# Rounding the next tile's rows earlier in the expert loop of a conv-attention-MoE kernel, and keeping its results later

## What is computed

```
router_logits = jnp.einsum('bsd,de->bse', x, Wg)
top_logits, top_idx = jax.lax.top_k(router_logits, TOP_K)      # TOP_K = 2
...
for e in range(E):                                             # E = 8
    h = jax.nn.silu(xt @ W1[e]) @ W2[e]                        # W1[e]: 128x512, W2[e]: 512x128
    out = out + cw[:, e:e + 1] * h
```

## Time and profile before

| | |
|---|---|
| median of three runs | 745.14 us (742.14 to 745.18) |
| profiled execution, its own time | 746.05 us |
| its span, first to last instruction | 744.2 us |
| TensorE matmul busy | 610.9 us (82%) |
| VectorE, ScalarE, GpSimd busy | 473.7, 306.3, 266.3 us |
| first matmul of the experts | 551.64 us |
| last scatter issued | 722.34 us |

### The profile page before, as it was taken

The page is one execution under the profiler, slowest core; times in us unless marked ns, Lnnn a source line. Parts: engine busy times, 40 slices in busy tenths (PEclk is TensorE's granted clock), DMA queues, the critical chain, the costliest instruction groups (busy, mean ns, idle before and its releaser), DMA issues. The chain is left out here.

```text
span 744.2 us, 11191 instructions
## 1 busy us (share of the span) xinstructions
PE 610.9 (82%) x3561; PEld 517.6 (70%) x3561; DVE 473.7 (64%) x1216; ACT 306.3 (41%) x615; POOL 266.3 (36%) x292
## 2 busy tenths in 40 slices
PE   5699999748699999989897997986229999999930
PEld 4588888535498898978796887875127777777720
DVE  5576795756558687857577686674305666666625
ACT  3221211242345363525344343432017777777810
POOL 3041553476000101321314141224632666666660
PEclk9899999859789999999899997887559999999985
DMA  8999434520441312130503122000177676777109
GB/s 263 386 362 334 170 133 165 177 92 1 141 142 54 89 60 83 57 115 5 167 1 126 46 85 87 19 12 25 37 236 244 215 234 210 228 224 235 62 5 337
DMA packets 56375, 105.47 MB, mean 142 GB/s; under 512 B 8872, under 2 KB 21817, under 8 KB 56192
## 3 DMA queue, kind: packets, MB, share of 16 engines
q1 hardware_dynamic: 51328, 96.24, 39.6%
q0 software_dynamic: 4992, 8.54, 3.3%
HBM read 58.15 MB, written 48.42 MB: 143 GB/s over the span
## 5 line engine op out<-in xcount | busy, mean ns | idle before, releaser
L1481 PE MATMUL bank<-rvx,s_expd 128*128 128x96 f32 x1024 | 139.5, 284 | 11.4 <-ACT s_expd L995 9.4
L1481 PEld LDWEIGHTS bank<-rvx,s_expd 128*128 128x128 f32 x1024 | 132.7, 202 | 14.5 <-ACT s_expd L995 11.3
L1744 POOL DMA_INDIRECT y_slots<-virt,pad_l x92 | 101.3, 1101 | 75.3 <-DVE virt L1795 47.5
L995 ACT ACTIVATE s_expd<-bank 128x512 f32<-128x512 f32 x128 | 75.7, 598 | 124.6 <-PE bank L1465 109.2
L1157 DVE TENSOR_REDUCE s_max<-bank 128x2 f32<-128x512 f32 x128 | 87.1, 689 | 57.3 <-PE bank L1444 44.7
L914 POOL DMA_INDIRECT x_slots<-rows,slot_of x64 | 62.7, 980 | 72.1 <-DVE rows L1284 48.2
L883 POOL TENSOR_TENSOR ln_rstd<-ln_var,power 128x4 f32<-128x4 f32 x16 | 16.4, 1022 | 199.0 <-DVE ln_var L1133 199.0
L1783 DVE TENSOR_TENSOR k_stack<-virt,k_stack 128x512 fp32r<-128x512 f32 x92 | 62.7, 688 | 18.1 <-ACT k_stack L1763 9.2
L53 PE MATMUL bank<-pad_h,u_h 128*128 128x512 f32 x144 | 60.9, 423 | 14.7 <-DVE pad_l L395 8.3
L1465 PE MATMUL bank<-q_stack,k_stack 100*128 100x256 f32 x256 | 62.4, 328 | 5.2 <-DVE q_stack L1175 5.2
L1763 ACT ACTIVATE k_stack<-virt 128x512 fp32r<-128x512 f32 x92 | 58.1, 632 | 2.9
(11 more groups left out here) (251 smaller groups left out, 1241.0 us busy)
## 6 DMA issues: line engine op xcount, KB each, us to landing
x_slots<-blank SPq DMA_DIRECT2D x8, 2112.0 KB, 20.4
pad_h<-w_split SPq DMA_DIRECT2D x23, 512.0 KB
q_stack<-w_split SPq DMA_DIRECT2D x23, 512.0 KB
qk_rows<-qk SPq DMA_DIRECT2D x16, 512.0 KB
k_stack<-qk_rows SPq DMA_DIRECT2D x96, 64.0 KB, 2.2
q_stack<-qk_rows SPq DMA_DIRECT2D x48, 128.0 KB, 2.4
pad_l<-x_slots SPq DMA_DIRECT2D x23, 264.0 KB
e_raw<-in_w SPq DMA_DIRECT2D x16, 256.0 KB, 3.0
```

The costliest lines, as they stand in the source:

```text
L995: nc.scalar.activation(expd[:, s % 2].rearrange("p a i -> p (a i)"), ps_st[s % 2][:, :], ACT.Exp).then_inc(exp_done, 1)
L1481: last = pe.matmul(ps_pv[s // 4][:, at:at + RVW], expd[:, s % 2, a, i * P:(i + 1) * P], rvx[:, ring, 2 * b + a, :], start=(a == 0), stop=( ...
L1744: pool.indirect_dma_start(out=y_slots[:, :], out_offset=bass.IndirectOffsetOnAxis(ap=ids, axis=0), in_=y_rows[:, t % 2, j, :], in_offset=N ...
```

## The change

Two orders are rewritten; TensorE's, GpSimd's and SyncE's stay as they are, and no operation is added or taken away. ScalarE rounds the rows of tile t+1 between silu(t, 1) and high(t, 1), where before it rounded those of tile t+2 after high(t, 1). VectorE's subtraction follows it. `keep_y(t - 1)` moves from behind low(t, 0) to ahead of low(t, 3). What stood behind low(t, 2) as `weigh(t - 1)` now stands one turn of the loop later, as `weigh(t - 2)` behind low(t, 1).

```diff
@@ ScalarE @@
         for t in range(NB):
             for f in range(FB):
                 silu(t, f)
+                if f == 1 and 1 <= t < NB - 1:
+                    z_split(t + 1)
                 high(t, f)
-                if f == 1 and t + 2 < NB:
-                    z_split(t + 2)
@@ VectorE @@
         for t in range(NB):
             for f in range(FB):
+                if f == 1 and 1 <= t < NB - 1:
+                    z_rest(t + 1)
+                if f == 3 and t:
+                    keep_y(t - 1)
                 low(t, f)
-                if f == 0 and t:
-                    keep_y(t - 1)
-                if f == 1 and t + 2 < NB:
-                    z_rest(t + 2)
-                if f == 2 and t:
-                    weigh(t - 1)
+                if f == 1 and t >= 2:
+                    weigh(t - 2)
+        weigh(NB - 2)
         keep_y(NB - 1)
         weigh(NB - 1)
```

## The result

The change takes 737.01 us in the median of four runs (735.71 to 738.04), the kernel before 745.16 in four (742.14 to 748.87). The ratio is 0.988, with a 95% interval of 0.985 to 0.991: 8.15 us faster, where 8.5 had been forecast. The profiled execution took 735.71 us, its span is 733.8.

What follows compares the result with a forecast made beforehand. TensorE was taken as the bound, with small holes where ScalarE waited for same-round transposes. Gains of 8.7 and 0.7 less 0.86 made 8.5 us, so 736.6 us, range 734.0 to 741.0 without the rivals.

Steps and rivals of the forecast that it cites:

- The chain: In expert rounds, ScalarE's wait for a same-round transpose delays silu, high and low, leaving TensorE holes of 0.33 and 0.30 us.
- The rounds: Rounds 1 to 20 of the experts: 6.40 us each without holes, 128.0 instead of 136.70, gaining 8.7 us.
- The start: Round 0 falls from 6.73 to about 5.9 to 6.0 us, gaining 0.7.
- I count nothing for that, at worst 0.5: Round 1's start may wait for the first moved rounding and its subtraction: counted as nothing, at worst 0.5 us.
- The tail: After the last rounds, weigh(20) comes later behind low(21, 1), delaying the twelve scatters and everything behind: 0.86 us lost.
- The sum: Whole kernel: 8.7 + 0.7 - 0.86 = 8.5 us gained, giving a median of 736.6 us.
- GpSimd as the bound: Experts' scatters all lengthened by colliding lows, 6.84 us a tile, making the kernel slower at 751.0 us; chance 0.04.
- Low(t, 3) behind the copy: VectorE's low(t, 3) stays late behind keep_y, a 0.30 us hole every round, only 2.5 gained, 742.6 us; chance 0.07.
- third rival: ScalarE stays in its old phase, subtraction ends late, each round's first product waits: slower, 760 us; chance 0.03.
- ScalarE's rest: ScalarE's line takes 5.48 us of a 6.40 us round, leaving 0.9 us of rest to catch up with.

Runs made afterwards that it cites:

- the other pattern of before: Unchanged kernel before, profiled again on another chip: every round 6.71 us, nineteen in 127.47 against 129.99 in the first profile; that execution took 723.7 us.
- the rounding alone: Kernel before with only ScalarE's rounding and VectorE's subtraction moved as in the change, keep_y and weigh left in place: 770.33 us, ratio to before 1.033.
- the results alone: Kernel before with only keep_y and weigh moved as in the change, rounding and subtraction left at tile t+2: 780.29 us, ratio to before 1.044.
- five more copies: The change plus five extra ScalarE copies into an unused buffer ahead of each rounding from tile 2 on: 737.81 us, ratio to before 1.024.

## Why the prediction was right

**The chain.** Shown. The step "ScalarE was made to wait for a transpose of the same round" is confirmed from both sides: the waits went from 23 to 2, and moving the same wait elsewhere, with the tile unchanged, brought rounds of 6.4 too, though not all. "That the rounding is one tile less ahead" was never the cause.

**The rounds.** 6.40 us were forecast, 6.41 came. The timeline of the change has the starts of rounds 0, 1 and 21, which answer to the earlier trace rows:

```profile
556.89 0.39 PE L53 MATMUL bank<-k_stack,pad_h 128*128 128x512 f32 x1
...
563.03 0.50 PE L53 MATMUL bank<-k_stack,pad_h 128*128 128x512 f32 x1
...
691.22 0.39 PE L53 MATMUL bank<-k_stack,pad_h 128*128 128x512 f32 x1
```

Rounds 1 to 20 take 691.22 - 563.03 = 128.19 us where 128.0 was forecast and 136.70 measured before: 8.51 gained, where the term was 8.7. But part of it was luck of the profile I read: in the other pattern of before, it would have been 0.30 a round, 6.1 in all, and a forecast of some 739.

**The start.** "I count nothing for that, at worst 0.5": the subtraction of tile 2 ended at 562.97 and up(2, 0) started at 563.03, 0.15 later than the pace of matmuls would have had it. Round 0 took 6.14 instead of 6.73: 0.59 gained, where the term was 0.7; what is missing is about this wait. The 0.98 of the table, from turn_z(1) to turn_z(3), is not to be set beside that term: this stretch also holds the rise of the granted clock from 1.2 to 2.4 GHz, whose moment varies (turn_z(1) to turn_z(2) took 6.42 and 6.51 in two profiles of before, 5.94 and 6.04 in two of the change).

**The tail.** The forecast counted from the start of round 21, since round 20 is in the term above. From there to weigh(20) it is 706.08 - 702.72 = 3.36 us before and 695.48 - 691.22 = 4.26 with the change: 0.90 lost, where the term was 0.86. (The table's 0.60 begins at turn_z(22), inside round 20, and holds 0.30 of that round's gain.) The step that everything behind hangs on weigh(20) holds in the change, but with only 0.22 of room left. Not forecast was that 0.20 is won back behind weigh(20): the twelve scatters hold 0.63 of lengthening before (1.29 and 1.30 instead of 0.98) and 0.43 with the change (1.31 and 1.08).

**The sum.** 8.51 + 0.59 - 0.90 + 0.20 = 8.40 us from the start of round 0 to the last scatter, where 8.7 + 0.7 - 0.86 = 8.5 was forecast. Every term came out, each within 0.2. The other 2.0 between the two spans are no effect that was forecast: 1.9 ahead of the experts, 0.5 from their first matmul to round 0, in which the clock rises, and 0.4 lost at the end. The two medians, 8.15 apart, are nearer to the sum, but their interval, some 7 to 11 us, would have held other sums too.

**The rivals.** GpSimd as the bound did not come: in round 7 it stood idle for 1.35, and none of its scatters there took more than 1.06. Low(t, 3) behind the copy did no harm either, and ScalarE got ahead. But the third rival's mechanism, the round's first product waiting for its subtraction, is exactly what the rounding alone ran into; there it was not ScalarE that was late but VectorE's line.

**ScalarE's rest.** The 0.9 us came from adding up durations. Its operations overlap (0.48 from start to start for a copy of 0.60), and the rest is 1.4. The forecast used the 0.9 only against rival 3, where more rest makes the argument stronger.

## What to carry to other kernels

In an engine's hand-written line, ask of each wait whose work stands behind it: the wait for something of this round must not stand ahead of an operation that the bottleneck wants in this round. Two moves may each be a loss and together a gain, so an order is to be judged whole; and where one engine's line is to run a round ahead of the other's, every operation in it must ask only for what was made a round ago. Count an engine's rest by distances from start to start, not by durations, and look at a second execution before taking an alternating pattern for the kernel's own.

## What the hardware showed that I had not expected

- **The granted clock can fall in the middle of a steady stage.** In the kernel with the results alone TensorE stood idle for 1.8 us in each round. Most rounds took 8.42 us, but two in a row took 10.05 and 10.04. The table of stretches shows the granted clock at 0.83 in them, the mean of 2.4 GHz and a part at 1.2, and 1.00 on both sides:

```profile
651.00:659.80 8.80, 6.98 (x35) 5.48 (x34) 4.54 (x7) 5.07 (x9) 4.08 (x5) 1.00 0.62 185
659.80:669.80 10.00, 8.19 (x33) 6.48 (x32) 4.47 (x7) 5.06 (x9) 4.45 (x4) 0.83 0.51 157
669.80:679.90 10.10, 8.28 (x33) 6.41 (x32) 4.54 (x7) 5.07 (x9) 3.93 (x4) 0.83 0.50 158
679.90:688.00 8.10, 6.28 (x32) 5.01 (x31) 4.47 (x7) 5.07 (x9) 3.19 (x4) 1.00 0.57 178
```

  The kernel with five more copies did the same once: TensorE stood 1.89 us ahead of round 1, and the clock was 0.80 over that round, which took 8.48 us. Why only these rounds, among many with the same hole, isn't shown. In the kernel with the rounding alone, with 1.38 of idle time in every round, it did not happen.

- **A scatter loses the rest of the low it starts in.** The one at 611.14 had 0.55 of a low ahead of it and took 1.41 instead of 0.98; in the change one at 602.98 had 0.20 ahead and took 1.06. Both lost 0.12 less than the rest, and so did all 257 scatters in the fourteen profiles that start with 0.14 to 0.65 of a low left, within 0.01. That is nearer than I had allowed to what the Trainium skill, page "SBUF — State Buffer", section "SBUF: two separate sides", states of an exclusive lock that the second comer waits for. The other half of that rule does not show here: a low that started at 602.49, inside a scatter (601.66 to 602.68), took its usual 0.69, and so did 60 others in the change (0.68 to 0.70). Only low, whose two inputs both lie in SBUF, lengthens a scatter. One that starts inside a subtraction, a copy or a weighing, which read PSUM, takes 0.98 to 1.00, with up to 0.69 of that operation left. And where a low starts 0.03 to 0.04 us ahead of the scatter, as it does in 16 rounds of the kernel with the results alone, the scatter takes its 0.98 and the low 0.76.
- **The same program differed by 30 us between chips** (720.28 to 750.51 us in the median). Two profiles of before have spans 22.2 us apart, and 20.2 of these lie ahead of the experts, whose first matmul started at 551.64 in one and at 531.48 in the other. Only ratios within one chip are compared here.
